# Cross-attention and table-weight FFN on one core: another source for the head norms' factor in the first batch, and the first index chunks, transfers and look-ups one place earlier

## Chip, cores and metric

The kernel runs on one core of one Trainium2 chip. The metric is device time in microseconds (us): the median over runs of the slowest core, here the only one. Lower is better.

## Reference, cut to what matters

Input x is (4, 512, 512), the context (4, 512, 256), all float32. Each batch does:

```
q  = LN_head((LN(x) @ Wq + bq) in 16 heads of 32) * w + b          # LN over the 32 values of a head
k  = LN_head(y[:496] @ Wk + bk), v = y[:496] @ Wv + bv
kd = LN_head(y[496:] @ Wkv_dca[:, :512] + b), vd = y[496:] @ Wkv_dca[:, 512:] + b   # 16 extra keys
x  = x + (softmax(q k^T / sqrt(32)) v + softmax(q kd^T / sqrt(32)) vd) @ Wo + bo
h  = silu(LN(x) @ lut[gate_idx]^T) * (LN(x) @ lut[up_idx]^T)       # lut has 16 values
x  = x + h @ lut[down_idx]^T                                        # inner size 1376
```

The FFN weights exist only as indices into a table of 16 values. The kernel looks them up once, while it works on the first batch.

## The kernel before

**Tiles and stages.** A batch has T = 4 row tiles of 128. Products use each float32 operand as a float16 high half and low half (three matmuls for one). Each engine has a program of its own, an order written out by hand; the engines meet only in counting semaphores. `core(a, ...)` is one batch of attention: projections and head norms, then stage one (scores and row maxima, slots S_ONE + 0 to 31, two slots to a *pair*), the shift (S_SUM, S_SHIFT), and stage two (transposed scores, exponentials, weighted values, slots S_TWO + 0 to 15). In later batches the FFN of the batch before fills the slots. In batch 0 there is no such FFN: `prepare(slot)` puts there what makes the FFN weights.

**Setup of batch 0.** Nine units in the order q0, q1, k1, k2, k3, d, k0, q2, q3 (`UNITS_0`; d is the extra keys of all batches in one unit of 64 rows). A unit u goes: `project(u)` on TensorE, `square(u)` on ScalarE (L865), `variance(u)` on VectorE (L1248, the sum over each head), `rstd(u)` on GpSimd (L701, the power -1/2 on 128x16 values), `normalise(u)` on VectorE (L1258), `turn_heads(u)` on TensorE (L1898, four transposes), `rescale(u)` on ScalarE (L886, L887), `low_half(u)` on VectorE (L1270). `project(u)` for u from 3 on waits for `normalise(u - 3)`, whose PSUM bank it takes. The values have `project_values(i)`. The weights are centred over each head and split on ScalarE and VectorE (L1552 makes low halves); so are the d weights, in `extra_sums`, `extra_centre`, `extra_low` (L1616, L1621, L1552) and the d context (`cd`).

**The look-ups.** The indices are 11 blocks of 3 chunks, 33 in all (`NCH`); 16 (`NQ`) is the number of stage-one pairs. A block is loaded as int32, cast to float16 on GpSimd (`convert`, L617), stored to DRAM (`store_idx`), and read back in four-fold copies (`load_rep`, L419, three buffers; `load_rep(c)` waits until `one_hot(c - 3)` is done). `one_hot(c)` is four compares on VectorE, one to a quarter (L1141), into four buffers of which each waits for the look-up before to have read it. `look_up(c)` is 32 matmuls on TensorE (L1750), eight to a quarter. `lookup_out(c)` is two copies on ScalarE (L819, L820). In stage one's pair i VectorE compares chunk i, TensorE looks up chunk i - 1 and ScalarE copies it out. In pairs 4 to 15 TensorE also makes `early` products of the next batches, which ScalarE copies out (`early_out`, L851, L854) before TensorE goes on. Chunk 15 is compared a quarter in pair 15, a quarter at S_SUM and two at S_SHIFT; TensorE looks it up in stage two's first slot, two chunks behind the compare. Chunks 31 and 32 are looked up inside the next batch's projections (`LATE`). The low half of Wo is made at S_SHIFT + 1, ahead of the compare of chunk 16 (L1552, four instructions).

**Queues.** Nearly all transfers go by SP in program order; a wait there holds back all behind it.

## Time and profile before

| | |
|---|---|
| median of 3 runs | 805.92 us (805.81 to 806.84) |
| the profiled execution | 806.87 us, its span 805.1 us |
| TensorE busy | 757.8 us of the span |
| VectorE, ScalarE, GpSimd busy | 513.0, 491.7, 264.8 us |
| mean granted TensorE clock | 0.989 |

The profile comes from one execution. Its span lies 1.8 us under that execution's own time, which lies 0.95 us over the median. Busy shares are averages over the whole span; the stages of batch 0 (roughly the first 205 us) have other limits than the rest, so they are read stage by stage.

### The profile page before, as it was taken

How to read it: one execution, taken by the hardware profiler on the slowest of the kernel's cores; microseconds unless marked ns; L12 is line 12 of the kernel's file. 1: busy time of each engine (PE TensorE's matmuls, PEld its weight loads, DVE VectorE, ACT ScalarE, POOL GpSimd, SP SyncE). 2: the span in 40 equal slices, each digit the busy share in tenths (PEclk: the TensorE clock that was granted, in tenths of full speed). 3: DMA queues.
4: the chain of work that ended last, by engine and by line, in shares of the span. 5: the costliest groups of instructions: out<-in, count | busy, mean ns of one | idle time of the engine just before them, and what ended most of it. 6: DMA issues, size and time to landing. Idle time of an engine off the chain costs nothing.

```text
span 805.1 us, 14839 instructions
## 1 busy us (share of the span) xinstructions
PE 757.8 (94%) x5833; PEld 310.6 (39%) x5833; DVE 513.0 (64%) x991; ACT 491.7 (61%) x1001; POOL 264.8 (33%) x276
## 2 busy tenths in 40 slices
PE   2888786999999999999999999999999999999998
PEld 1342232333443343324443342235433433365445
DVE  7979999898877994225769953228499800153211
ACT  3479889788646886662658866636488855511100
POOL 6883221000763321113843321035622210014320
PEclk9998999899999999999999999999999999999999
DMA  7749997586430001221500003222000000100001
GB/s 255 195 126 268 259 259 214 140 188 156 125 81 1 1 2 33 74 53 59 122 6 1 2 15 78 54 66 54 2 1 1 1 28 27 41 14 1 0 14 40
DMA packets 74389, 61.49 MB, mean 76 GB/s; under 512 B 33424, under 2 KB 60816, under 8 KB 74064
## 3 DMA queue, kind: packets, MB, share of 16 engines
q1 hardware_dynamic: 73984, 60.29, 28.2%
q8 instruction: 46, 0.75, 0.4%
q10 hardware_dynamic: 208, 0.26, 0.1%
q14 instruction: 23, 0.19, 0.1%
q0 software_dynamic: 128, 0.00, 0.0%
HBM read 43.55 MB, written 10.55 MB: 67 GB/s over the span
## 4 chain that ended last, share of the span: by engine, by line
PE 77%; DVE 13%; ACT 3%; POOL 3%; issue 3%; DVEq 0%; POOLq 0%; ACTq 0%
PE ps L1699 51%; PE ps L2050 8%; PE ps L2031 6%; PE ps L2002 5%; PE ps L1750 5%; DVE arena L1141 4%; DVE nmax L1494 3%; POOL hrstd L701 2%; PE ps L2037 2%; ACT ps L1024 2%; PE ps L1898 2%; DVE nmax L1499 1%; DVE stat L1178 1%; DVE arena L1148 1%; POOL xrstd L645 1%
## 5 line engine op out<-in xcount | busy, mean ns | idle before, releaser
L1699 PE MATMUL ps<-arena,wf_hi 128*128 128x512 f16 (+2 forms) x736 | 211.0, 371 | 0.7 <-issue 0.7
L1024 ACT ACTIVATE ps<-ps,nmax 128x496 f32<-128x496 f32 x256 | 166.1, 652 | 23.3 <-DVE nmax L1499 23.3
L1056 ACT ACTIVATE arena<-ps 128x1024 f32<-128x1024 f32 x128 | 124.3, 1026 | 72.1 <-PE ps L2037 72.1
L1699 PE MATMUL ps<-arena,wf_lo 128*128 128x512 f16 (+2 forms) x368 | 136.1, 370 | 0.0
L1699 PE MATMUL ps<-wf_hi,arena 128*128 128x512 f16 (+3 forms) x374 | 114.8, 368 | 0.5 <-DVE arena L1148 0.2
L701 POOL TENSOR_TENSOR hrstd<-hvar,mhalf 128x16 f32<-128x16 f32 (+1 forms) x33 | 100.8, 3068 | 39.5 <-DVE hvar L1248 39.4
L1699 PEld LDWEIGHTS ps<-arena,wf_hi 128*128 128x128 f16 (+1 forms) x736 | 69.5, 100 | 85.8 <-issue 21.5
L1141 DVE TENSOR_SCALAR arena<-arena,wf_lo 128x2048 f16<-128x2048 f16 (+1 forms) x132 | 89.5, 739 | 5.6 <-PE ps L1750 5.4
L1750 PE MATMUL ps<-arena,wf_lo 128*32 128x512 f16 (+1 forms) x1056 | 66.4, 396 | 13.5 <-ACT arena L851 9.5
L645 POOL TENSOR_TENSOR xrstd<-xvar,mhalf 128x1 f32<-128x1 f32 x32 | 23.8, 743 | 158.5 <-DVE xvar L1183 158.5
L1699 PE MATMUL ps<-wf_lo,arena 128*128 128x512 f16 (+3 forms) x187 | 68.5, 366 | 0.0
L2050 PE MATMUL ps<-arena 128*32 128x512 f32 x512 | 68.2, 604 | 0.0
L1699 PEld LDWEIGHTS ps<-wf_hi,arena 128*128 128x128 f16 (+1 forms) x374 | 36.4, 97 | 74.0 <-issue 39.5
L827 ACT ACTIVATE arena<-ps 128x512 f32<-128x512 f32 (+1 forms) x44 | 26.1, 594 | 62.1 <-PE ps L1699 62.1
L1499 DVE TENSOR_REDUCE nmax<-ps 128x1 f32<-128x496 f32 x96 | 63.8, 665 | 0.0
L1500 DVE TENSOR_REDUCE nmax<-ps 128x1 f32<-128x496 f32 x96 | 63.8, 665 | 0.0
L1161 DVE SCALAR_TENSOR_TENSOR arena<-ps,arena 128x512 f32<-128x512 f32 x15 | 10.4, 692 | 83.1 <-PE ps L1699 83.1
L576 POOL TENSOR_TENSOR idle<-mhalf 128x1 f32<-128x1 f32 x44 | 8.9, 202 | 151.2 <-DVE arena L1156 151.2
L2002 PE MATMUL ps<-arena 32*128 32x512 f16 x768 | 53.6, 382 | 3.6 <-ACT ps L1024 2.0
L1148 DVE SCALAR_TENSOR_TENSOR arena<-arena,ps 128x512 f32<-128x512 f32 (+1 forms) x44 | 30.0, 682 | 39.1 <-ACT arena L827 39.1
L2031 PE MATMUL ps<-arena 32*128 32x512 f16 x768 | 53.5, 381 | 0.0
L1024 ACT ACTIVATION_READ_ACCUMULATOR ps<-ps,nmax 128x1 f32 x256 | 53.3, 208 | 0.0
(154 smaller groups left out, 1049.1 us busy)
## 6 DMA issues: line engine op xcount, KB each, us to landing
arena<-idx SPq DMA_DIRECT2D x124, 128.0 KB, 3.6
arena<-in_x SPq DMA_DIRECT2D x32, 256.0 KB, 2.9
wf_lo<-in_idx SPq DMA_DIRECT2D x10, 512.0 KB, 5.3
idx<-wf_hi SPq DMA_DIRECT2D x10, 384.0 KB, 4.4
out<-arena SPq DMA_DIRECT2D x15, 256.0 KB, 2.1
wf_lo<-in_idx SPq DMA_DIRECT2D x11, 256.0 KB, 6.8
arena<-in_ctxT SPq DMA_DIRECT2D x5, 512.0 KB, 3.8
v_next<-arena SPq DMA_DIRECT2D x8, 256.0 KB, 4.5
```

The costliest lines, as they stand in the source:

```text
L701: pool.tensor_tensor(hrstd[0:n_, u % 2, :], hvar[0:n_, u % 2, :], mhalf[0:n_, :], ALU.pow).then_inc(s["hrstd_set"], 1)
L1024: last = act.activation(sc, sc, ACT.Exp, bias=nmax[:, 0, t, h:h + 1], accum_out=den[:, 0, t, h:h + 1])
L1056: act.activation(probs[n_ % 2][:, 2 * p:2 * p + 2, :], ps[:, bank:bank + 2, :], ACT.Exp).then_inc(s["probs_set"], 1)
L1141: dve.tensor_scalar(l_oh[q][:, 0:n_], l_rep[c % REPS][:, 0:n_], l_j[:, q:q + 1], None, ALU.is_equal)\
L1148: dve.scalar_tensor_tensor(out=g, in0=g, scalar=1.0, in1=ps[0:m, ffn_bank(f, it), :], op0=ALU.add, op1=ALU.mult)\
L1499: dve.tensor_reduce(nmax[:, 0, t, 2 * p:2 * p + 1], sc[:, 0:1, DCA:S], AX_X, ALU.max, negate=True).then_inc(s["max_set"], 1)
L1500: dve.tensor_reduce(nmax[:, 0, t, 2 * p + 1:2 * p + 2], sc[:, 1:2, DCA:S], AX_X, ALU.max, negate=True)\
L1699: last = pe.matmul(dst, l, r, start=(first and i == 0), stop=(stop and i == len(todo) - 1))
L1750: last = pe.matmul(ps[g * 32:(g + 1) * 32, FB + a_, 0:w], l_c[a_][:, q, :], l_oh[q][:, g * w:(g + 1) * w], start=(q == 0), stop=(q == NJ - ...
L2002: last = pe.matmul(ps[:, pair_bank(m + j // 2) + j % 2, :], qT[x_][of_head(j), g, cols], kT[y_][of_head(j), g, :], start=(k == 0), stop=(k ...
L2031: pe.matmul(ps[:, SC + j, :], kT[x_][of_head(j), g, cols], qT[y_][of_head(j), g, :], start=(k == 0), stop=False)
L2050: last = pe.matmul(ps[j * HD:(j + 1) * HD, pv_bank(g), :], v_sb[:, kt, h * HD:(h + 1) * HD], probs[n_ % 2][:, j, :], start=(kt == 0), stop ...
```

## The change

Head norms of units 0 to 6 in batch 0: VectorE takes the reciprocal of the sum (`inverse`), ScalarE the root (`root`); GpSimd keeps units 7 and 8. An `Exp` on one value stands before `rescale(7)` in ScalarE's order. The d unit is no longer split: its product is made from the float32 weights and the float32 context, and the mean over a head is taken from the product in PSUM. `one_hot(0)` moves into the setup, so every compare, look-up and copy-out of stage one handles a chunk one higher; chunk 15 is looked up at S_SHIFT, and stage two's look-ups run one chunk behind the compare. Wo is transferred once the d products are made, blocks 1 and 2 are cast and stored before the last projection, Wo's low half moves into stage two's first two slots. The written orders of the setup change on all four engines. In the diff below, calls that stand on lines of their own are joined on one line, and long arguments are cut.

```diff
-LATE = {AHEAD: NCH - 2, AHEAD + 1: NCH - 1}
+LATE = {AHEAD + 1: NCH - 1}
...
@@ SP
-            sp.wait_ge(s["wd_lo"], 1)
-            sp.dma_start(st_o..., by_chunk("Wo")).then_inc(s["wo_in"], 16)
...
             load_rep(2)
+            sp.wait_ge(s["proj_done"], UNITS_0.index(("d", 0)) + 1)
+            sp.wait_ge(s["v_done"], values_of((0, 0)).index(("d", 0)) + 1)
+            sp.dma_start(st_o..., by_chunk("Wo")).then_inc(s["wo_in"], 16)
+            store_idx(1)
+            store_idx(2)
             sp.wait_ge(s["proj_done"], nth_unit((0, 0), len(UNITS_0)))
             sp.dma_start(ctx_early...)
-            store_idx(1)
...
@@ GpSimd, setup
-                    rstd(0)
+                    norm(1, 0, (0, 0)); selectors(); norm(1, 1, (0, 0)); norm(1, 2, (0, 0))
                     convert(0)
-                    for u in range(1, len(units)):
-                        rstd(u)
+                    norm(1, 3, (0, 0))
                     convert(1)
+                    lookup_constants(); shift_patterns()
+                    convert(2)
+                    rstd(7)
+                    rstd(8)
                     low_half(a, 7, 0)
-                    convert(2, 1)
-                    context_low(2)
-                    convert(3, 3)
+                    convert(3, 2)
+                    context_low(3)
                     convert(4, 4)
                     convert(5, 5)
                     dca_shift(a, 0, 6)
                     low_half(a, 8, 6)
...
@@ ScalarE
+            def root(u):
+                n_ = MD if UNITS_0[u][0] == "d" else P
+                act.wait_ge(s["inv_set"], u + 1)
+                if u >= 2:
+                    act.wait_ge(s["qn_set"], u - 1)
+                act.activation(hrstd[0:n_, u % 2, :], hinv[0:n_, u % 2, :], ACT.Sqrt).then_inc(s["hrstd_set"], 1)
...
-                    act.activation(wd[0][:, :, :], st_d, ACT.Copy, scale=WS).then_inc(s["wd_hi"], 1)
...
+                    values(4)
+                    act.activation(warm[:, :], mhalf[:, 0:1], ACT.Exp)
                     rescale(7)
...
-                            lookup_out(c - 1)
+                            lookup_out(c)
+                if slot == S_ONE + 1:
+                    lookup_out(0)
...
                 if slot >= S_SHIFT + 1:
-                        lookup_out(c - 2)
+                        lookup_out(c - 1)
@@ VectorE
+            def inverse(u):
+                ...
+                dve.reciprocal(hinv[0:n_, u % 2, :], hvar[0:n_, u % 2, :]).then_inc(s["inv_set"], 1)
...
                     variance(a, 0)
                     context_lo(a, ctx_first, cT)
-                    value_bias(); key_low(); standardise(1, 2, ...); extra_context_low()
+                    inverse(0)
+                    moments(1, 2, a, x_first[2])
                     variance(a, 1)
                     normalise(a, 0, True)
-                    values_low(); variance(a, 2); extra_sums(); extra_centre(); parameters()
+                    inverse(1); standardise(1, 2, ...); parameters(); variance(a, 2)
                     normalise(a, 1, True)
+                    inverse(2)
                     variance(a, 3)
-                    extra_low()
                     normalise(a, 2, True)
+                    moments(1, 3, a, x_first[3]); inverse(3); variance(a, 4); inverse(4); low_half(0)
+                    normalise(a, 3, True); extra_centre(a); low_half(1); turn(1, 2, ...); standardise(1, 3, ...)
+                    low_half(2); normalise(a, 4, True); variance(a, 5); inverse(5); low_half(3)
+                    normalise(a, 5, True); turn(1, 3, ...); variance(a, 6); inverse(6); low_half(4)
+                    one_hot(0, (0,)); variance(a, 7); one_hot(0, (1,)); low_half(5); normalise(a, 6, True)
+                    one_hot(0, (2,)); (d keys into kT); variance(a, 8); value_bias(); normalise(a, 7, True)
+                    low_half(6); one_hot(0, (3,))
...
+            def extra_centre(a):
+                u = units_of(a).index(("d", 0))
+                kd_ps = heads(ps[0:MD, proj_bank(a, u), :])
+                dve.wait_ge(s["proj_done"], nth_unit(a, u + 1))
+                dve.tensor_reduce(sum_d, kd_ps, AX_X, ALU.add).then_inc(s["kd_sum"], 1)
+                dve.wait_ge(s["kd_sum"], 1)
+                dve.scalar_tensor_tensor(out=kd_ps, in0=spread(sum_d), scalar=-1.0 / HD, in1=kd_ps, ...).then_inc(s["kd_cent"], 1)
...
             def prepare(slot):
-                if slot == S_SHIFT + 1:
-                    (low half of Wo, g = 0 to 3)
                 for c in lookups_in(slot):
-                    if c < NCH - 1:
-                        one_hot(c, (0,) if c == NQ - 1 else range(NJ))
+                    if c < NQ - 2:
+                        one_hot(c + 1)
+                    elif c == NQ - 1:
+                        one_hot(c, (0,))
+                    elif NQ <= c < NCH - 1:
+                        one_hot(c)
+                if slot in (S_TWO, S_TWO + 1):
+                    (low half of Wo, two of the four g in each)
@@ TensorE
-                        keys = [(both(lambda a_: cd[a_][:, i, :]), both(lambda a_: wd[a_][:, i, 0:D])) for i in range(KC)]
+                        keys = [(ctx_dca[:, i * MD:(i + 1) * MD], st_d[:, i, 0:D]) for i in range(KC)]
...
+                    turn(1, 0, ...); turn(1, 1, ...); project(0); project(1)
+                    project_values(0)
                     project(2)
+                    project_values(1)
                     project(3)
-                    project_values(0)
                     turn(1, 2, a, LB0[2], x_first[2])
-                    project_values(1)
                     turn_heads(0)
                     project(4)
                     turn_heads(1)
-                    project_values(2)
                     project(5)
                     turn_heads(2)
+                    project_values(2); project(6); turn_heads(3)
                     project_values(3)
                     turn(1, 3, a, LB0[3], x_first[3])
-                    turn_heads(3); project(6)
                     turn_heads(4)
                     project(7)
...
                 for c in lookups_in(slot):
-                    if slot < S_SUM and c:
+                    if slot < S_SUM and c < NQ - 1:
+                        look_up(c)
+                    elif slot >= S_TWO:
                         look_up(c - 1)
-                    elif slot >= S_TWO:
-                        look_up(c - 2)
+                if slot == S_SHIFT:
+                    look_up(NQ - 1)
```

## Rows read from the trace of the kernel before

**Rows 1.** Windows of batch 0: busy time of each engine, granted clock (PEclk), DMA share, GB/s
```profile
40.00:60.00 20.00, 16.22 (x93) 8.44 (x91) 15.50 (x27) 15.25 (x28) 18.30 (x8) 0.94 0.42 123
...
100.00:120.00 20.00, 17.04 (x207) 6.26 (x206) 19.99 (x27) 17.83 (x54) 4.65 (x4) 1.00 0.97 262
...
160.00:180.00 20.00, 20.00 (x312) 7.45 (x308) 18.72 (x35) 17.49 (x26) 1.12 (x2) 1.00 0.88 184
```

**Rows 2.** Groups by line on GpSimd, 0 to 56 us
```profile
L701 POOL TENSOR_TENSOR hrstd<-hvar,mhalf 128x16 f32<-128x16 f32 (+1 forms) x9 | 29.6, 3302 | 1.4 <-DVE hvar L1248 1.3
```

**Rows 3.** Timeline of VectorE, setup and first pair: start, duration, line, idle before
```profile
24.66 1.22 DVE L1221 TENSOR_TENSOR arena<-arena 128x1024 f16<-128x1024 f32 x1
...
29.28 1.85 DVE L1552 SCALAR_TENSOR_TENSOR wv<-arena,wv 128x1024 f16<-128x1024 f32 x1
...
31.67 1.20 DVE L1616 TENSOR_REDUCE arena<-arena 128x32 f32<-128x1024 f32 x1
32.91 1.29 DVE L1621 SCALAR_TENSOR_TENSOR arena<-arena 128x512 f32<-128x512 f32 x2
...
36.20 2.28 DVE L1552 SCALAR_TENSOR_TENSOR wd<-arena,wd 128x2048 f16<-128x2048 f32 x1
...
55.67 1.19 DVE L1494 TENSOR_REDUCE nmax<-ps 128x2 f32<-128x992 f32 x1 [1.08 <-PE ps L2002]
...
61.75 2.29 DVE L1494 TENSOR_REDUCE nmax<-ps 128x2 f32<-128x992 f32 x2 [0.41 <-PE ps L2002]
```

**Rows 4.** Timeline of TensorE: products of the setup, a head turn, float32 products
```profile
27.25 1.46 PE L1699 MATMUL ps<-wk,arena 128*128 128x512 f16 x6
28.54 0.38 PE L1699 MATMUL ps<-b,sel_k 128*128 128x512 f16 x1
...
37.26 0.60 PE L1898 MATMUL ps<-ident,arena 128*128 128x128 f32 x4
...
45.65 2.75 PE L1699 MATMUL ps<-wq,arena 128*128 128x512 f16 x12
...
147.55 1.06 PE L2050 MATMUL ps<-arena 128*32 128x512 f32 x8
...
151.25 1.06 PE L2050 MATMUL ps<-arena 128*32 128x512 f32 x8
```

**Rows 5.** Timeline of ScalarE: d weights, a small copy, the table load after stage one
```profile
34.24 1.91 ACT L991 ACTIVATE wd<-arena 128x2048 f16<-128x2048 f32 x1 [0.91 <-DVE arena L1621]
...
56.90 0.20 ACT L1018 ACTIVATE arena<-ps 128x32 f32<-128x32 f32 x1 [0.64 <-DVE nmax L1494]
...
137.85 1.28 ACT L1034 ACT_TABLE_LOAD   x1
```

**Rows 6.** Timeline of TensorE, look-ups of stage one
```profile
61.57 3.25 PE L1750 MATMUL ps<-arena,wf_lo 128*32 128x512 f16 x32
...
88.98 1.91 PE L1750 MATMUL ps<-arena,wf_lo 128*32 128x512 f16 x32 [2.23 <-ACT arena L851]
...
129.80 1.91 PE L1750 MATMUL ps<-arena,wf_lo 128*32 128x512 f16 x32 [0.90 <-ACT arena L851]
...
134.78 1.91 PE L1750 MATMUL ps<-arena,wf_lo 128*32 128x512 f16 x32 [0.90 <-ACT arena L851]
```

**Rows 7.** Timeline of ScalarE, the copy-out of the third early product
```profile
88.33 0.60 ACT L851 ACTIVATE arena<-ps 128x512 f32<-128x512 f32 x1 [1.22 <-POOL arena L666]
```

**Rows 8.** Timeline of VectorE: a chunk's compare, a standardise, the next batch's first residual
```profile
130.65 2.73 DVE L1141 TENSOR_SCALAR arena<-arena,wf_lo 128x2048 f16<-128x2048 f16 x4
...
175.77 0.55 DVE L1188 TENSOR_SCALAR arena<-arena,mv,xrstd 128x512 f32<-128x512 f32 x1 [0.67 <-POOL xrstd L645]
...
210.43 0.69 DVE L1215 SCALAR_TENSOR_TENSOR arena<-ps,arena 128x512 f32<-128x512 f32 x1 [0.54 <-PE ps L1699]
```

**Rows 9.** Timeline of TensorE, the first FFN product of the next batch
```profile
232.06 0.59 PE L1699 MATMUL ps<-arena,wf_hi 128*128 128x512 f16 x2 [0.74 <-issue]
```

**Rows 10.** Windows of TensorE around the shift: busy time, granted clock, DMA share, GB/s
```profile
139.00:146.00 7.00, 5.03 (x48) 0.53 0.41 116
```

204 lines of the change are left out of this document (106 added, 98 removed).

## Prediction

> **What bounds the kernel now.** I read the busy times of windows first, because every edit lies in batch 0 and the page's shares are means over all batches. Three limits follow each other. In the setup (to 55.67 us, the first row maximum [rows 3]) no engine is full but GpSimd: 18.3 of 20 us between 40 and 60, against 15.5 on VectorE, 15.25 on ScalarE, 16.2 on TensorE [rows 1]. The groups by line say with what: nine powers for the head norms, 3.3 us each, 29.6 us together [rows 2]. In stage one VectorE is full (19.99 of 20), with ScalarE at 17.8 and TensorE at 17.0 close behind [rows 1]. From stage two on TensorE is full (20.00 of 20), VectorE at 18.7 [rows 1]. What ends the setup or stage one sooner therefore moves all that comes later; what takes work from VectorE in stage two is worth nothing; what takes TensorE work out of stage two or the next batch is worth its length, unless something else is late there.
>
> **Setup: the powers.** Seven of nine go from GpSimd to a reciprocal and a root. No row shows either. For the reciprocal the rows bound it between 0.1 us (next to nothing on 16 values) and 0.6 (half the reduce over 1024 values, 1.20 [rows 3]); I take 0.15, seven make 1.0. The root works on 16 values and stands between nothing and the 0.20 of the copy of 32 [rows 5]; I take 0.15. The GpSimd queue (7 x 3.3 = 23 us in a row) is then gone, and the question is what is late next. Two lists compete, TensorE's and VectorE's, both from the moment the context's low half is made: 24.66 + 1.22 = 25.9 now [rows 3]. In the new order nearly the same instructions stand ahead of it (two moments fewer, about 1.0 each; the low halves of values and keys more, 1.1 each), so I keep 25.9 to 26.3.
>
> TensorE, from there: a product of six float16 matmuls takes 28.54 - 27.25 = 1.3, with the bias 1.5; one of twelve 2.75, with bias 2.8 less overlap; four head transposes 0.60, of which 0.44 count when others follow [rows 4]. The d product becomes float32. Float32 matmuls of 512 columns show only four side by side, a quarter of the array each: 1.06, less the 0.17 of tail that 1.46 has over 1.29, 0.89 [rows 4]. One that fills the array takes 0.22 if those four run one after another and 0.89 if they run at once; I take 0.88, so two are 1.76 in place of 1.3, for keys and values each. The other bound makes the d unit 2.6 us cheaper than that. The list: four value products 5.2, four key products 6.0, two queries 5.6, d 1.97 + 1.76, two turns 0.9, eight head turns 3.5: 24.9 us. It ends at 26.1 + 24.9 = 51.0, and with the scores (0.8) the first maximum is at 51.8 at the soonest.
>
> VectorE, from there: eight variances and eight normalises at 0.6 (9.7), seven reciprocals 1.0, two moments 2.0, two standardises 0.9, parameters 0.9, seven low halves 3.9, the d mean in PSUM 1.25, two turns 1.2, the four compares of chunk 0 at 2.73 / 4 = 0.68 less overlap [rows 8] 2.65, copies 0.3: 23.9 us, so 49.8 without a wait. What left it: 1.20 + 1.29 + 2.28 for the d weights [rows 3] and 0.3 for the d context. ScalarE loses 1.91 [rows 5] and gains seven roots and two table loads. Walking the three orders together, VectorE waits 1.1 for the square of unit 3 (TensorE has that product at 26.1 + 1.3 + 1.5 + 1.3 + 1.5 = 31.7) and about 1.5 for units 7 and 8, and TensorE never waits longer than 0.5: both lists meet at 52.5. Blocks 1 and 2 are now cast on GpSimd inside the setup, beside VectorE: the one cast there now made the values' low half 1.85 where an instruction of the same size took 1.22 [rows 3]. Two more casts and the pattern copies cost 0 to 2.5 by this; some fall beside PSUM reads, I take 0.5. The first maximum: 53.0 in place of 55.67, **-2.7 us**. Bounds: 51.8 (-3.9) and, if VectorE's waits and collisions add instead of hiding each other, 55.0 (-0.7).
>
> The Trainium skill (ScalarE: Activation LUTs, "What ACT_TABLE_LOAD costs") puts a switch of table set at 2.66 us with its drain. The trace has 1.28 for the load [rows 5]. The first switch falls in a gap of ScalarE of 2.6 us either way; the second, ahead of `rescale(7)`, would by the page cost the first pair 1.4 us more and make the sum 1.4 smaller.
>
> **First pair.** `look_up(0)` now stands between the last head turn and the second scores. Maximum to next maximum is 61.75 - 55.67 = 6.1 us with a wait of 0.41 for the scores, which themselves waited for `rescale(8)` [rows 3]. If the look-up takes 1.91 it hides there (-0.4); at the clock that the first look-up has now, 3.25 [rows 6], compares and scores come 1.5 later. I take 0.
>
> **Stage one, a chunk higher.** The compare, the look-up and the copy-out keep their distances, so a pair is what it was. VectorE loses a whole chunk (2.73) in the fifteenth pair. That is not 2.7 us: look-ups start 134.78 - 129.80 = 4.98 us apart, TensorE waiting 0.90 for ScalarE's early copy each time [rows 6], and this loop (look-up, copy-out, exponentials, early copy, next look-up) is as long as VectorE's own pair. At the end ScalarE's last exponentials and the table load at 137.85 [rows 5] gate the shift as now. Value of the missing compare: **0**, at most -0.5.
>
> One stall goes. The third early copy waits 1.22 us on ScalarE for GpSimd's low half of unit 8 [rows 7], which stands behind `dca_shift(a, 0, 6)`: six chunks compared. TensorE therefore waits 2.23 instead of 0.90 before the look-up at 88.98 [rows 6]. Six chunks are now compared one pair (about 4.9 us) sooner, which covers the 1.22 fully: **-1.35 us**. The waits at later chunks keep their slots.
>
> **The sixteenth chunk and stage two.** `look_up(15)` goes from stage two into the shift, where TensorE is idle anyway. In stage two 16 look-ups stay, one of them of 384 columns instead of 512 (-0.4), and in the next batch's projections the look-up of chunk 31 (1.4 us) goes. There the gain is not whole: before the first FFN product TensorE already waits 0.74 [rows 9] for the transposed rows, at the end of a VectorE list without a gap but one, 0.54 before its first residual [rows 8]. TensorE can only win what that list wins: -0.55.
>
> Against it: with one chunk of lead instead of two, VectorE must finish the compare for slot n + 1 while it has its other work of slot n. A slot is 151.25 - 147.55 = 3.70 us [rows 4]; a chunk 2.65; a standardise comes 0.67 late after GpSimd [rows 8]. Counting slot by slot (a compare may start 2.4 us into the slot and must start by 4.3), slots 1, 4 and 10, where a standardise stands ahead of the compare, and the two with Wo's low halves (1.25 each) miss it, by 0.4 + 0.15 + 0.6 + 0.5 = 1.7. Stage two's present waits (0.5, from the same standardises) go: +1.2. Bounds 0 and, if each slot missed by 0.3, +4.8. Stage two: -0.4 + 1.2 = **+0.8**, the next batch **-0.55**.
>
> **The clock.** From 139 to 146 the granted clock is 0.53 [rows 10], nearly 1.2 GHz, after TensorE had stood idle for the shift; slot 0's products pay 2.4 us for it (a look-up 3.25 against 1.91 [rows 6] is 1.35 of that). The new order puts 1.8 us of look-up, in four pieces, into that idle time. I do not count on it: 0, bound -2.4.
>
> **Transfers.** Wo (1 MB), blocks 1 to 4 and a context now queue on SP between 42 and 50 us; ScalarE wants the context in the first pair. The present queue at 40 to 60 is at 0.42 of the engines [rows 1]; cover is the rest. 0, and 1 us if the context lands late.
>
> **Sum.** -2.7 + 0 - 1.35 + 0.8 - 0.55 = -3.8. The profiled execution took 806.87 us (span 805.1); it should take 803.1. The median, 0.95 below it, goes from 805.92 to **802.1**.
>
> **Rivals.**
> A, the clock holds: `look_up(15)` keeps TensorE at 2.4 GHz through the shift. -3.8 - 2.4: 799.7. For it: its four pieces leave no gap over 1.5 us. Against: 1.8 us of look-up in about 7 from the last early product to the shift's transposes. 0.13.
> B, the setup is not GpSimd's: VectorE's list with casts and waits ends at 55, the lead lost in stage two costs 2 to 3. -0.7 - 1.35 + 2 - 0.55 = -0.6: 805.3. For it: three engines at 15 to 16 of 20 [rows 1], and the 0.6 us that one cast cost VectorE [rows 3]. 0.15. The Trainium skill (SBUF — State Buffer, "SBUF: two separate sides") says that of a VectorE instruction with two SBUF inputs and a GpSimd instruction the later one is locked out until the other is done; the trace agrees (1.85 against 1.22). By that rule casts placed beside VectorE's list are dear, and it is what B would come from.
> C, slower: the table thrashes. If square, copy or identity is not in the root's table set, each of roots 0 to 6 brings a load before and after. The point from which it decides is the first square after a root. Twelve loads of 1.28 [rows 5] in place of two are 12.8 us more on an engine with about 10 idle between 23 and 54, and each root stands in the chain to a normalise: +8 on the setup. -3.8 + 8: 810.1. Against: squares and copies now run beside exponentials with no load between. 0.07. The Trainium skill (ScalarE: Activation LUTs, "Table sets: the hidden batching unit") puts exponential and root in different sets and asks to batch calls by set; it also has the cheap functions in every set, which speaks against C.
> That the change does not do what it says (the powers stay in the chain): units 7 and 8 are still powers; if `normalise(8)` became the end it would cost under 1 us, inside the forecast.
>
> **Chances and range.** Forecast 0.65, A 0.13, B 0.15, C 0.07. The range reaches past A to 799.2 (0.5 of the 1.2 that the setup's best bound has over its value), and to 806.2 past B (0.9 more of stage two's bound); outside are C and the tails. The forecast's own range is 800.5 to 804.5. A change of 0.2% (1.6 us) is about what a measurement tells. Faster by more (below 804.3): the forecast but for its upper tail 0.60, A 0.13, B 0.05: 0.78. Within: 0.12. Slower (C and a bad stage two): 0.10.
>
> **What would show it.** First row maximum at 52 to 54 (right), 55 or later (B). No GpSimd power before unit 7. One table load before the first root and one before `rescale(7)`, not more (else C). The third early copy without a wait for GpSimd. Look-ups 4.98 apart in pairs 5 to 15. Short waits of TensorE for compares in slots 1, 4 and 10, each under 1 us; if every slot has one, the stage two term is wrong. The wait before the first FFN product grows from 0.74 to about 1.6. The granted clock at the shift near 0.5 (else A). The forecast fails if the setup's float32 products take over 1.76 a pair, or if the reciprocal is over 0.3.

## The result, and the profile after

The changed kernel takes 808.3 us (median of 18 runs, 806.32 to 809.16); the kernel before, run beside it on the same chip, 806.52 us (18 runs, 805.30 to 807.96). The ratio is 1.0018, interval [1.0012, 1.0024]. Forecast were 802.1 us and a range up to 806.2: the time moved the other way and lies outside the range. The profiled execution took 809.01 us, with a span of 807.2 us and a mean granted clock of 0.992.

The points below are starts of the same instruction in both traces; they add up to the two spans (us).

| stretch | before | after | difference | forecast |
|---|---|---|---|---|
| start to first row maximum | 55.67 | 56.89 | +1.22 | -2.7 |
| first to second row maximum | 6.08 | 8.00 | +1.92 | 0 |
| second maximum to the shift's transposes | 79.22 | 77.91 | -1.31 | -1.35 |
| transposes to the scores of stage two's second slot | 5.61 | 4.37 | -1.24 | 0 |
| second slot to the next batch's first query product | 56.42 | 58.86 | +2.44 | +0.8 |
| that product to the first FFN product | 29.06 | 28.31 | -0.75 | -0.55 |
| first FFN product to the end | 573.04 | 572.86 | -0.18 | 0 |
| sum | 805.1 | 807.2 | +2.1 | -3.8 |

The windows of the changed kernel that answer to [rows 1] and [rows 10] (busy time of TensorE, its weight loads, VectorE, ScalarE, GpSimd, then granted clock, DMA share, GB/s):

```profile
40.00:60.00 20.00, 17.25 (x97) 8.42 (x99) 18.87 (x33) 16.30 (x32) 13.78 (x12) 0.95 0.84 235
...
160.00:180.00 20.00, 19.90 (x300) 6.89 (x296) 18.35 (x34) 17.23 (x26) 1.12 (x2) 1.00 1.06 185
...
139.00:146.00 7.00, 5.69 (x64) 1.59 (x68) 6.06 (x14) 5.54 (x10) 0.00 (x0) 0.76 0.41 112
```

In the setup GpSimd went from 18.3 to 13.8 of 20 us and VectorE from 15.5 to 18.9: the fullest engine is another one now. In stage two TensorE is at 19.90 instead of 20.00.

TensorE's timeline says more (start, duration, line; in brackets the idle time before and who ended it):

```profile
27.66 2.72 PE L1725 MATMUL ps<-wv,arena 128*128 128x512 f16 x6 [3.33 <-DVE arena L1241]
30.17 1.68 PE L1725 MATMUL ps<-wk,arena 128*128 128x512 f16 x6
...
37.62 1.93 PE L1725 MATMUL ps<-arena 128*64 128x512 f32 x4
...
58.74 1.12 PE L1924 MATMUL ps<-ident,arena 128*128 128x128 f32 x4 [1.95 <-DVE arena L1285]
59.78 3.60 PE L1776 MATMUL ps<-arena,wf_lo 128*32 128x512 f16 x32
```

and its windows in the same columns as above:

```profile
26.00:28.00 2.00, 0.34 (x1) 0.14 (x2) 2.00 (x4) 0.59 (x3) 0.00 (x0) 0.80 0.00 0
28.00:30.00 2.00, 2.00 (x6) 0.73 (x5) 1.92 (x8) 0.41 (x1) 1.29 (x2) 0.50 0.01 4
...
58.00:60.00 2.00, 1.26 (x8) 0.86 (x12) 1.78 (x3) 1.73 (x7) 1.16 (x1) 0.50 1.10 290
```

Twice TensorE stands idle, 3.33 and 1.95 us, and twice the granted clock is then 0.50, that is 1.2 GHz. The first value product takes 2.72 us where its like in [rows 4] took 1.46, the key product behind it 1.68, and the look-up that was moved between turn and scores takes 3.60.

The same places in the trace of before:

```profile
24.19 2.76 PE L1699 MATMUL ps<-wq,arena 128*128 128x512 f16 x12 [0.90 <-DVE arena L1206]
...
57.52 1.12 PE L1898 MATMUL ps<-ident,arena 128*128 128x128 f32 x4 [1.95 <-DVE arena L1258]
60.17 1.47 PE L2002 MATMUL ps<-arena 32*128 32x512 f16 x12 [1.54 <-ACT arena L887]
...
143.31 3.33 PE L1750 MATMUL ps<-arena,wf_lo 128*32 128x512 f16 x32
```

There the second query product filled the time up to the first key product at 27.25; in the first pair TensorE idled just as long, but the second scores (60.17) stood ahead of the look-up; and the look-up of stage two's slot 0 took 3.33.

VectorE in the same stretch, beside GpSimd's casts:

```profile
27.43 0.25 DVE L1275 RECIPROCAL hinv<-hvar 128x16 f32<-128x16 f32 x1
...
35.54 0.70 DVE L1268 TENSOR_REDUCE hvar<-arena 128x16 f32<-128x528 f32 x1 [1.35 <-ACT arena L870]
...
38.83 1.61 DVE L1297 TENSOR_TENSOR arena<-arena 128x512 f16<-128x512 f32 x1
...
46.02 1.14 DVE L1297 TENSOR_TENSOR arena<-arena 128x512 f16<-128x512 f32 x1
...
56.89 1.19 DVE L1529 TENSOR_REDUCE nmax<-ps 128x2 f32<-128x992 f32 x1 [0.42 <-PE ps L2032]
...
64.89 2.29 DVE L1529 TENSOR_REDUCE nmax<-ps 128x2 f32<-128x992 f32 x2 [0.69 <-PE ps L2032]
```

```profile
38.43 1.46 POOL L620 CAST wf_hi<-wf_lo 128x1536 f16<-128x1536 int32 x1
...
45.16 1.46 POOL L620 CAST wf_hi<-wf_lo 128x1536 f16<-128x1536 int32 x1
```

The low half of a unit is one instruction (L1297), mostly of 0.68 us; it takes 1.61 and 1.14 where a cast of GpSimd lies beside it. From 36 to 56 us VectorE waits only once, for 0.39 us.

ScalarE's tables, and the third early copy (before: [rows 7]):

```profile
25.01 1.28 ACT L878 ACT_TABLE_LOAD   x1
27.71 0.22 ACT L878 ACTIVATE hrstd<-hinv 128x16 f32<-128x16 f32 x1 [1.41 <-DVE hinv L1275]
...
55.34 1.28 ACT L1028 ACT_TABLE_LOAD   x1
56.64 0.20 ACT L1028 ACTIVATE warm<-mhalf 128x1 f32<-128x1 f32 x1
...
90.10 0.65 ACT L854 ACTIVATE arena<-ps 128x512 f32<-128x512 f32 x1
```

Besides a load at 3.67 us that both kernels have, the setup has these two loads, none between roots and squares. The third early copy no longer waits. TensorE's look-ups then show the stall leave, stage two pay, and the next batch's wait grow (before: [rows 6, 9]):

```profile
90.80 1.91 PE L1776 MATMUL ps<-arena,wf_lo 128*32 128x512 f16 x32 [0.90 <-ACT arena L854]
...
144.65 2.51 PE L1776 MATMUL ps<-arena,wf_lo 128*32 128x512 f16 x32 [0.30 <-DVE arena L1161]
...
153.38 2.51 PE L1776 MATMUL ps<-arena,wf_lo 128*32 128x512 f16 x32 [0.48 <-DVE arena L1161]
...
234.34 0.59 PE L1725 MATMUL ps<-arena,wf_hi 128*128 128x512 f16 x2 [1.52 <-issue]
```

At a granted clock of 1.00 a look-up of 32 products takes 1.91; 2.51 is one that waits inside for the quarters of a compare (in slot 2 the compare ends at 155.23, the look-up at 155.89). Slots 0, 2, 5 and 11 have 2.51, slots 3, 9 and 13 have 2.06 to 2.16. VectorE shows what stands ahead of such a compare:

```profile
152.03 0.55 DVE L1208 TENSOR_SCALAR arena<-arena,mv,xrstd 128x512 f32<-128x512 f32 x1 [0.67 <-POOL xrstd L648]
152.49 2.74 DVE L1161 TENSOR_SCALAR arena<-arena,wf_lo 128x2048 f16<-128x2048 f16 x4
```

### The profile page after: what moved, and what is told of

Read it like the earlier page. It is cut to its first block, busy times and chain, and to the rows that moved or that the text cites. A ratio compares the mean times of both kernels' runs of the same rounds, so it can differ in the third digit from the quotient of the medians.

```text
span 807.2 us, 14844 instructions
## 1 busy us (share of the span) xinstructions
PE 759.8 (94%) x5829; PEld 308.6 (38%) x5829; DVE 512.3 (63%) x995; ACT 494.1 (61%) x1010; POOL 238.7 (30%) x269
## 4 chain that ended last, share of the span: by engine, by line
PE 71%; DVE 17%; ACT 5%; issue 3%; DMA 2%; POOL 1%; SPq 1%; DVEq 0%
PE ps L1725 50%; PE ps L2080 7%; DVE arena L1161 6%; PE ps L2061 5%; PE ps L2032 5%; ACT ps L1042 2%; DVE nmax L1529 2%; PE ps L1776 2%; PE ps L2067 1%; PE ps L1924 1%; DMA arena<-in_x 1%; DVE stat L1198 1%; DMA v_next<-arena 1%; DVE nmax L1534 1%; DVE hvar L1268 1%
## 5 line engine op out<-in xcount | busy, mean ns | idle before, releaser
L706 POOL TENSOR_TENSOR hrstd<-hvar,mhalf 128x16 f32<-128x16 f32 x26 | 76.7, 2964 | 45.9 <-DVE hvar L1268 45.6
L648 POOL TENSOR_TENSOR xrstd<-xvar,mhalf 128x1 f32<-128x1 f32 x32 | 20.1, 629 | 179.8 <-DVE xvar L1203 179.8
L830 ACT ACTIVATE arena<-ps 128x512 f32<-128x512 f32 (+1 forms) x44 | 26.1, 594 | 63.0 <-PE ps L1725 63.0
```

The lines of the kernel that those rows point to most:

```text
L706: pool.tensor_tensor(hrstd[0:n_, u % 2, :], hvar[0:n_, u % 2, :], mhalf[0:n_, :], ALU.pow).then_inc(s["hrstd_set"], 1)
```

## The experiments

Ratios are to the kernel before in the same session. "Filler" is a product of float16 weights into a bank that nobody reads then; it adds work and no result. Runs of one kernel spread over 2 to 3 us, so a difference of one trace is set against the medians.

| run | median us | ratio to before, interval |
|---|---|---|
| changed kernel | 808.30 | 1.0018 [1.0012, 1.0024] |
| e1 filler in the first pair | 806.53 | 0.9994 [0.9985, 1.0004] |
| e4 filler in the setup | 805.79 | 0.9986 [0.9977, 0.9995] |
| e6 both | 804.70 | 0.9978 [0.9969, 0.9987] |
| e3 stage two in the old order | 807.38 | 1.0003 [0.9993, 1.0013] |
| e2 powers in the new order | 820.44 | 1.0167 [1.0152, 1.0182] |
| b2 roots in the old order | 813.26 | 1.0089 [1.0074, 1.0104] |
| e5 constants early | 807.33 | 1.0012 [1.0002, 1.0021] |
| b1 five chunks, before | 806.15 | 0.9992 [0.9984, 1.0001] |
| b3 fillers before, misplaced | 812.50 | 1.0077 [1.0063, 1.0091] |
| b4 fillers before | 804.69 | 0.9980 [0.9971, 0.9989] |
| b5 b4 and five chunks | 804.37 | 0.9975 [0.9965, 0.9985] |
| c1 first combination | 803.51 | 0.9969 [0.9956, 0.9981] |
| c2 second combination | 801.95 | 0.9947 [0.9934, 0.9959] |
| c3 c2 and constants early | 802.46 | 0.9951 [0.9937, 0.9965] |

### The clock in the first pair (e1), in the setup (e4), both (e6)

```diff
                     project(1)
+                    for k_ in range(14):        # e4 and e6
+                        pe.matmul(ps[:, FB, :], wq[0][:, k_ % KQ, 0:P], wq[0][:, k_ % KQ, :], start=True, stop=True)
                     project_values(0)
...
                     if prev is None and m == 0:
+                        for k_ in range(9):     # e1 and e6
+                            pe.matmul(ps[:, FB + 1, :], wq[0][:, k_ % KQ, 0:P], wq[0][:, k_ % KQ, :], start=True, stop=True)
                         turn_heads(8)
```

> The changed kernel with nine float16 matmuls of no use put on TensorE between the first scores and the head turn of unit 8, into bank 7, where it stood idle for 1.95 us. Theory (clock): the second row maximum comes 8.0 us after the first because the look-up of chunk 0, now on the path, runs at 1.2 GHz (3.60 us) after that idle time; kept busy, the look-up takes 1.91 and the distance falls to 6.1 to 6.5, the time by 1.5 to 1.9 us. Rival (order): the look-up ahead of the second scores costs the same wherever the clock stands, distance 7.5 or more, time changed by less than 0.5 us.

> The changed kernel with fourteen float16 matmuls of no use on TensorE (bank 6) in its idle 3.3 us before the first value product. Theory (clock): that product takes 1.46 instead of 2.72 us, squares 2 and 3 come 1.4 us sooner, VectorE's waits of 0.91 and 1.35 us for them shrink, and the first row maximum comes at 55.5 instead of 56.89. Rival (VectorE's list): its list is full from 36 us on and takes the waits back, so that the maximum stays at 56.5 to 56.9 and the time as it is.

> The changed kernel with both fillers at once: 14 products without a use while TensorE waits ahead of the first value product, and 9 between the first scores and the turn of unit 8. Theory (TensorE's clock, which falls after each of the two waits, carries 1.4 us of the setup and 1.9 us of the first pair, and the two are independent): the gains add. First value product to first row maximum 27.8 us, first to second maximum 5.9, later stages as in the changed kernel; against the changed kernel -3.2, so 804.6 to 805.2 where the kernel before has 806.9: ratio 0.9975. Rival (a filler only moves a wait: VectorE's list ends the setup, and what TensorE wins in one place it waits in the next): first maximum not before 55.5, ratio 0.999 to 1.000.

TensorE's timeline in e1, then in e4:

```profile
55.75 2.12 PE L2043 MATMUL ps<-wq 128*128 128x512 f16 x9
57.77 0.66 PE L1924 MATMUL ps<-ident,arena 128*128 128x128 f32 x4
58.35 1.91 PE L1776 MATMUL ps<-arena,wf_lo 128*32 128x512 f16 x32
```

```profile
23.36 3.19 PE L1961 MATMUL ps<-wq 128*128 128x512 f16 x14
26.86 1.45 PE L1725 MATMUL ps<-wv,arena 128*128 128x512 f16 x6 [0.31 <-DVE arena L1241]
```

In e1 the turn takes 0.66 instead of 1.12, the look-up 1.91 instead of 3.60, and first to second maximum is 5.83 instead of 8.00 us (6.08 before): the first pair's loss is the clock. In e4 the first value product takes 1.45, and from it to the first maximum it is 27.78 us instead of 29.23. With both (e6) it is 27.78 and 5.83 again. So in the traces the two add, and the rival (won in one place, waited out in the next) falls. The medians lie 1.8, 2.5 and, with both, 3.6 us under the changed kernel's, which agrees within their spread. Extra work made the kernel faster.

What the clock leaves of the setup shows in e6, from the end of the context's low half to the end of VectorE's last compare of the setup (columns as in the windows above):

```profile
26.62:54.22 27.60, 26.58 (x139) 13.01 (x139) 25.93 (x55) 19.33 (x37) 15.56 (x15) 1.00 0.79 213
```

Of 27.60 us TensorE is busy 26.58 and VectorE 25.93. Both lists are full, and both are longer than the 24.9 and 23.9 us that the prediction gave them: VectorE's takes 26.3, and TensorE, from the first value product (26.85) to the first scores (53.70), is busy 26.06.

### Stage two in the old order (e3)

```diff
-LATE = {AHEAD + 1: NCH - 1}
+LATE = {AHEAD: NCH - 2, AHEAD + 1: NCH - 1}
...
                     elif slot >= S_TWO:
-                        look_up(c - 1)
+                        look_up(c - 2)
-                if slot == S_SHIFT:
-                    look_up(NQ - 1)
```

with the copy-outs one chunk later too, and Wo's low half back at S_SHIFT + 1.

> The changed kernel with stage two as before: chunk 15 looked up in its first slot, two chunks behind the compare, chunk 31 in the next batch, Wo's low half before the compare of chunk 16. Theory: the waits for late compares (2.4 us over the slots) go, the clock falls at the shift again (+1.2 us), and the next batch gets its 0.75 back: 0.5 us less in all. Rival (the lost lead costs nothing, the waits are there anyway): 1 to 2 us more.

```profile
141.96 0.58 PE L2049 MATMUL ps<-ident_h,caug 128*128 128x128 f16 x4 [7.10 <-DVE caug L1557]
...
144.30 2.59 PE L1776 MATMUL ps<-arena,wf_lo 128*32 128x512 f16 x32
...
148.68 1.91 PE L1776 MATMUL ps<-arena,wf_lo 128*32 128x512 f16 x32
```

Transposes to the next batch's first query product take 61.30 us here, 63.23 in the changed kernel and 62.03 before; from there to the first FFN product it is 0.77 us longer than in the changed kernel. The slots behind slot 0 have no late compare. The part moved in stage two costs about 1 us net, more than the +0.25 forecast for stage two and next batch together (+0.8 - 0.55) and more than the 0.5 expected of this run; its rival (1 to 2 us slower) falls. Slot 0 has to be read with care: its look-up took 3.33 in the trace of before, 2.59 here, and 2.60 in b1, which does the same as before there. The whole stretch is 5.61 in before and 4.71 in b1, so 0.7 to 0.9 us of its -1.24 is the spread from one execution to another.

### The norms alone: powers in the new order (e2), roots in the old one (b2)

```diff
# e2: in the changed kernel
-                    inverse(0) ... inverse(6)          (VectorE)
-                    root(0) ... root(6)                (ScalarE)
+                    rstd(0) ... rstd(6)                (GpSimd, among its norms and casts)
# b2: in the kernel before
                     variance(a, u)
+                    inverse(u)                         (VectorE, u = 0 to 6)
...
                     square(a, 3, True)
+                    root(2)                            (ScalarE, likewise the others)
-                    rstd(0); for u in range(1, len(units)): rstd(u)     (GpSimd)
+                    rstd(7); rstd(8)
```

> The changed kernel with the head norms of units 0 to 6 back as powers on GpSimd, without reciprocals, roots and the second table load; everything else, the order of VectorE's list too, as changed. Theory: the powers, seven of 3.3 us with casts and constants among them, are a queue of about 28 us from 27 us on, the first row maximum comes at 59 to 61, the time is 2 to 4 us more. Rival (the setup is bound by the other engines in the new order): it stays within 1 us of 56.9.

> The kernel before with one part of the change alone: the factor of units 0 to 6 by VectorE's reciprocal and ScalarE's root, in the old orders of the engines (units 7 and 8 stay powers; an Exp on one value stands ahead of the rescale of unit 7). The d unit, the compare of chunk 0, the transfers, the shift and stage two are as before. Theory (the nine powers were what ended the setup, 3.3 us apart; in the changed kernel it was the clock's fall after TensorE's idle 3.3 us and a full VectorE list of 26.3 us that took the gain): here VectorE has no compare of chunk 0 and TensorE no gap ahead of its key products, so the first row maximum comes at 53.5 to 54.5 where the kernel before has 55.7, the rest as before: ratio 0.998. Rival (the powers bound nothing, they were hidden behind the two other lists): first maximum 55.5 to 57, as VectorE has 1.8 us more in its list; ratio 1.000 to 1.002.

Both were misses: e2 lies 12 us over the changed kernel and b2 7 us over the kernel before, where +2 to +4 and -1.6 were expected. The waits of VectorE in the setup, of e2 and then of b2 (who waited for whom: total, times, longest):

```profile
DVE arena L1284 <- POOL hrstd L706: 11.0, 6, 2.8
DVE arena L1284 <- issue: 2.2, 1, 2.2
```

```profile
DVE arena L1294 <- ACT arena L896: 3.8, 3, 1.6
DVE hvar L1265 <- ACT arena L867: 3.5, 1, 3.5
```

In e2 VectorE waits for a power ahead of a normalise six times. GpSimd's list is why: from its first head-norm power to its last it is busy 37.91 of 42.73 us (25.67 to 68.40), where before it was busy 30.95 of 31.45 (24.82 to 56.27). The nine powers are the same, but the changed order puts three casts, two norms of x and the look-up constants among them; the old order had one cast there. The first seven with what stands among them were expected to take 28 us and took 33.7 (25.67 to 59.35), and the last two came behind one more cast. In b2 a root puts ScalarE itself into the chain: ScalarE waits for a reciprocal (1.82, 2.22 and 1.18 us), and the rescales queued behind the root are what VectorE then waits for. Where I put the roots among ScalarE's work was my choice, and a better place may exist; it was not tried. What is shown: the root is no gain in the old order as I placed it, the new order is none without the root, and only the two together come near the time of before.

### GpSimd beside VectorE (e5)

```diff
                     norm(1, 1, (0, 0))
+                    lookup_constants()
+                    shift_patterns()
                     norm(1, 2, (0, 0))
                     convert(0)
                     norm(1, 3, (0, 0))
                     convert(1)
-                    lookup_constants()
-                    shift_patterns()
```

> The changed kernel with one step moved on GpSimd: its look-up constants and shift patterns come ahead of the norms of tiles 2 and 3 and of the first two casts, so that from 36 to 50 us GpSimd has less beside VectorE. Theory (collisions of VectorE's copies with GpSimd's cost the setup about 1 us: 1.61 and 1.14 us where such instructions take 0.68): the pattern copies run beside VectorE's earlier, looser stretch, first maximum 0.5 to 1.0 earlier than in the changed kernel, ratio to it 0.999. Rival (the casts, not the patterns, collide, and they only come later now; the norm of tile 2 comes 3 us later and holds the query products back): first maximum the same or up to 1.5 us later, first value product later than 27.7, the time 0 to +1.5.

VectorE's low halves in e5:

```profile
38.88 1.61 DVE L1297 TENSOR_TENSOR arena<-arena 128x512 f16<-128x512 f32 x1
...
46.06 0.62 DVE L1297 TENSOR_TENSOR arena<-arena 128x512 f16<-128x512 f32 x1
```

The one at 46 us lost its 0.5 us of collision, the one at 38.9 (beside a cast) kept its 0.9. First value product to first maximum went from 29.23 to 28.99 (e1 and e3, without this edit, have 29.07 and 29.17). In the median e5 cannot be told from the changed kernel (the intervals overlap). The combination c1 shows where the rest goes: against e6 this stretch is 27.39 instead of 27.78, but the first value product starts at 27.25 instead of 26.85, because the standardise at 12.14, now beside GpSimd's constants and pattern copies, takes 0.94 instead of 0.54. The first maximum is at 54.64 in c1 and 54.63 in e6. The collision was moved, not removed, and the rival is nearer to what happened.

### The sixth chunk alone (b1)

```diff
-                    dca_shift(a, 0, 6)
-                    low_half(a, 8, 6)
+                    dca_shift(a, 0, 5)
+                    low_half(a, 8, 5)
```

> The kernel before with one step alone: GpSimd shifts and splits five chunks of unit 7 and 8 ahead of the early copy instead of six. Theory (ScalarE's third early copy waits 1.22 us for that step, and TensorE then 2.23 instead of 0.90): that wait is gone, second maximum to shift 1.3 us shorter (77.9 where the kernel before has 79.2), all else as before: ratio 0.9984. Rival (the sixth chunk comes late elsewhere, or the gain belongs to the chunks that moved up): 0 to +1, ratio 1.000 or above.

```profile
87.27 1.91 PE L1750 MATMUL ps<-arena,wf_lo 128*32 128x512 f16 x32 [0.90 <-ACT arena L851]
...
93.76 1.91 PE L1750 MATMUL ps<-arena,wf_lo 128*32 128x512 f16 x32 [1.84 <-ACT arena L851]
```

The stall at the third early copy is gone (0.90 instead of 2.23), but the next look-up comes 6.49 us later where it came 5.93 later before. Second maximum to transposes is 78.47 instead of 79.22: 0.75 of the 1.3 us that the whole change has there. The median moved by 0.4 us, which the interval does not separate from nothing; 1.3 us had been expected.

### Fillers in the kernel before (b3, b4, b5)

```diff
                 between(S_SHIFT)
+                pe.wait_ge(s["l_out"], NQ - 1)          # b3, 28 fillers in bank FB
+                pe.wait_ge(s["S_exp"], NS - 2)          # b4 and b5 instead, 18 fillers in bank TB
+                for k_ in range(28): ...
                 pe.wait_ge(s["S_exp"], nth(a, NS, NS))
```

and the 9 fillers of e1. b5 has the five chunks of b1 as well.

> The kernel before with fillers alone: 9 products without a use between the first scores and the turn of unit 8, and 28 ahead of the shift's transposes. It asks what the clock is worth without the change. Theory (before, the first pair hid the low clock behind VectorE's compare of chunk 0, so nothing is to be had there; only the shift pays, slot 0 at 5.1 us with a look-up of 3.3): first maximum 55.7, first to second maximum 5.8 to 6.1, transposes to second slot 3.8 to 4.1 instead of 5.6; 804.3 to 805.0, ratio 0.998. So the change with its clock held (the second combination, 801.95) keeps 2.5 to 3 us over this. Rival (the change brings nothing once the clock is taken out of both): 802 to 802.8, ratio 0.9955.

> The kernel before with fillers alone, in another place than the run before: 9 products without a use between the first scores and the turn of unit 8, and 18 right behind the sixteenth pair's look-up, in a bank that the exponentials have left, where TensorE idles 4.3 us ahead of the shift's transposes. Theory (the clock costs the old order about 2.2 us at the shift: from the transposes to the second slot 5.6 us, and 3.4 in the run before; and about 0.4 in the first pair, where VectorE's compare covers it): transposes at 140.4 to 140.7, second slot 3.4 to 3.8 later, 804.0 to 804.8, ratio 0.9975 to 0.998; the changed kernel with its clock held (801.95) then keeps 2 to 3 us from its own parts. Rival (the clock is all there is): 802.0 to 802.8, ratio 0.995 to 0.996.

> The kernel before with the fillers of b4 and GpSimd's early step on five chunks instead of six. Theory (the step alone took 0.75 us off stage one in its own run): 0.7 to 1.3 below b4, 803.0 to 804.0, ratio 0.9965; what is then left to the changed kernel with its clock held is 1 to 2 us, of setup and index order. Rival (the gain was the chance of that one run's profile): as b4, ratio 0.998.

TensorE in b3, then in b4:

```profile
140.38 7.90 PE L2021 MATMUL ps<-wq 128*128 128x512 f16 x28 [3.88 <-ACT wf_hi L820]
148.12 0.39 PE L2025 MATMUL ps<-ident_h,caug 128*128 128x128 f16 x4
```

```profile
137.73 4.06 PE L2021 MATMUL ps<-wq 128*128 128x512 f16 x18
142.08 0.38 PE L2025 MATMUL ps<-ident_h,caug 128*128 128x128 f16 x4 [0.29 <-DVE caug L1522]
...
143.36 1.91 PE L1750 MATMUL ps<-arena,wf_lo 128*32 128x512 f16 x32
```

b3 is my mistake: in the old order the copy that its fillers wait for comes only behind the shift, so they started when TensorE should have been done, and held the transposes back by some 7 us. It says nothing on its question. b4 puts them into the idle time: transposes to second slot 3.4 us instead of 5.6, first to second maximum 5.60 instead of 6.08, and 1.65 us off the median. That is what the clock costs in these two places of the kernel before. In b4's own trace the transposes come at 142.08, not at 140.4 to 140.7 as expected, because the look-up behind the third early copy, at 88.47, took 3.52 us. b5 takes the wait ahead of that look-up away (second maximum to transposes 78.85 instead of 80.82 in the two traces), but its median is only 0.3 us under b4's: short of the 0.7 expected, and with overlapping intervals, so nearer to its rival.

### The combinations (c1, c2, c3)

c1 is e6 with e5's edit and e3's; c2 is e6 with e3's edit and, as in b3, 28 fillers ahead of the shift's transposes (here the copy-out comes early enough); c3 is c2 with e5's edit.

> The changed kernel with four edits: both fillers of the clock, GpSimd's constants early, and stage two with the last index chunks in the old order (look-ups two chunks behind the compare, Wo's low half ahead of stage two). Theory: the fillers give 3.2 us, stage two in the old order 1.2, the constants 0 to 0.8, and they add, as they lie in different stages: 808.3 - 4.4 to 5.2 = 803.1 to 803.9, below the kernel before by 0.4% (ratio 0.996). Rival (the clock falls at the shift in any case once stage two is in the old order, and the gain of 1.2 is not on top of the fillers'): 804.5 to 805.3, ratio 0.9975, as with the two fillers alone.

> The changed kernel with both fillers of the setup and first pair, stage two and the last index chunks in the old order (GpSimd's constants where the changed kernel has them), and a third filler: 28 products without a use ahead of the shift's transposes, where TensorE idles 7.1 us in the combination before. Theory (slot 0 of stage two pays for the clock at 1.2 GHz after that idle time): granted clock near 1.0 at the shift, look-up of slot 0 at 1.9 instead of 2.57 us, transposes to second slot 3.8 instead of 4.85 us, so 1.0 to 1.5 us below the combination: 802.0 to 802.8, ratio to the kernel before 0.995. Rival (the fillers end before the transposes and TensorE waits for the shift's copies again, or they end late and hold the transposes back): slot 0 as in the combination or the transposes later, 803.5 to 804.5, ratio 0.997.

> The second combination (three fillers, stage two and the last index chunks in the old order) with GpSimd's constants early as well. Theory: the value from first value product to first maximum is 27.4 instead of 27.7, all else as in the second combination: 801.5 to 801.9, ratio 0.9943. Rival: the first value product starts 0.4 later with the constants early, as in the first combination, and the gain is gone: 801.9 to 802.4, ratio 0.9947.

TensorE in c2, and its window around the shift:

```profile
132.17 6.22 PE L2053 MATMUL ps<-wq 128*128 128x512 f16 x28 [0.90 <-ACT arena L854]
138.35 0.38 PE L2057 MATMUL ps<-ident_h,caug 128*128 128x128 f16 x4
...
139.64 1.91 PE L1776 MATMUL ps<-arena,wf_lo 128*32 128x512 f16 x32
```

```profile
139.00:146.00 7.00, 6.81 (x116) 2.60 (x108) 6.93 (x12) 5.34 (x7) 0.00 (x0) 1.00 0.40 106
```

c1 came as expected. c2 came just below its range: 801.95, 4.2 us under the kernel before and 6.4 under the changed one, the fastest version here. With the clock held in both orders, 801.95 stands against 804.69 (b4), or 0.9947 against 0.9980: the change's own parts, without its stage two, are worth 2 to 3 us. Against b5 (0.9975), which has the sixth chunk's part of them, 2.3 us are left. c2 has one filler more than b4, in the setup, where the trace of before has no gap ahead of its key product [rows 4]. c3 went as its rival said: 802.46, the first value product at 27.75 instead of 26.85 (0.41 of it a wait for x) and nothing gained over c2.

## Why the prediction was wrong

**"I keep 25.9 to 26.3" and the lists behind it: the step that failed first.** The new order makes the queries ready sooner, so the second query product ended at 24.33 us instead of 27.17; with both done, TensorE had nothing left and idled 3.33 us for VectorE's low half of the context. I counted its list from the end of that wait and never asked what it had done before. The two products behind that ran at 1.2 GHz, the second in part: 1.4 us (e4). The clock had a paragraph of its own, but only for the shift. The start itself was 0.7 us late too: the first value product comes at 26.85 in e4 and e6, for 26.1. The new order has VectorE wait 0.68 us for GpSimd ahead of the first standardise (at 7.09), where the old one had other work.

**VectorE's list.** Given 23.9 us, it took 26.3 in e6 (26.62 to 54.22, less waits of 0.91 and 0.39). Three terms carry it, read from start to start. Seven low halves took 5.3 us instead of 3.9, two of them beside casts. Seven reciprocals took 1.1 for 1.0 (0.16 apart), but a variance with a reciprocal behind it takes 0.72 instead of 0.61. Two standardises took 1.4 instead of 0.9. The collisions were costed at 0.5 us and came to about 2: 0.9 and 0.5 on two low halves, 0.5 on a standardise. Against that, VectorE's waits were 1.3 us where 2.6 were forecast. First value product to first maximum is then 27.8 us in e6, where the forecast had 26.9 (53.0 - 26.1): 0.9 more. The Trainium skill (SBUF — State Buffer, "SBUF: two separate sides") has the lock-out that the prediction weighed; the 1.61 us beside the cast at 38.43 agrees with it. It was rival B's mechanism, and it acted, together with a clock that B did not have.

**Float32 products.** Costed at 1.76 a pair; the keys' pair (four records) takes 1.77 from its start to the next product (37.62 to 39.39), the values' pair 1.86 (43.53 to 45.39): as forecast within 0.1. The 1.93 of the row includes the tail of the last product.

**The trace itself.** The changed kernel's profiled execution started its list 0.8 us late: VectorE waited 0.71 us for a tile of x at 8.94, which e3 did not (its first value product starts at 26.86, its first maximum at 56.03). Of the nine other traces with the changed order, seven have no such wait and two have 0.19 and 0.41. So the setup is +0.4 rather than +1.2 in most of the traces.

**First pair, forecast 0.** The bound of +1.5 for a look-up at 1.2 GHz stood in the text, and I took the other end. The rows held the answer: the old look-up of 3.25 in [rows 6] was slow after the same wait of 1.95 us (and one of 1.54). Before, the second scores (60.17) stood ahead of the look-up and came while VectorE compared chunk 0 (58.48 to 61.34), and the look-up ran beside the second maxima. So the low clock cost at most 0.5 us (6.08, with fillers 5.60 in b4). The change moved that compare away and put the look-up ahead of the second scores, which VectorE waits for: it took the cover off. With fillers (e1) the distance is 2.2 us shorter; 1.9 of that lay over the forecast.

**Stage one.** The stall (-1.31 for -1.35), the fifteenth pair's missing compare (worth 0), the distance of 4.98 us: right. The cause was only half right: b1 has 0.75 of it by the sixth chunk alone; the rest came with the other moves of index blocks, and which of them was not separated.

**Stage two, forecast +0.8.** The mechanism was right, the size not: seven slots were late, not five; six of them lie in this stretch and lose 0.15 to 1.26 us each, together 3.4 instead of 1.7; less the 0.5 of before and 0.4 of shorter look-up, +2.44. The slots behind a standardise, which I had named, lose most: 1.26, 0.75 and 0.72 us (look-ups of slots 2, 5 and 11). I let a compare start as late as 4.3 us into its slot because the look-up takes it in quarters. That was about 0.25 too generous: the compare at 179.52 starts 4.30 us behind the scores of its slot, and the look-up it feeds takes 2.16 for 1.91. And I did not count that VectorE makes a low half of the weighted values ahead of some compares, where it waits for ScalarE's high half (0.83 us ahead of slot 9's compare, 0.99 ahead of slot 13's).

**Clock at the shift, forecast 0 with -2.4 as rival A.** The window from 139 to 146 went from 0.53 to 0.76, part of A. Against b1's execution of the old order the stretch won 0.3 us, against before's 1.24; b4 and c2 show what all of it is worth, 2.2 us in that stretch.

**Next batch.** -0.75 for -0.55, and the wait ahead of the first FFN product grew to 1.52 as forecast.

**Rival C.** Only the two loads forecast appeared. The Trainium skill (ScalarE: Activation LUTs, "What ACT_TABLE_LOAD costs") adds a drain to the load; here the copy before the load ends at 55.33, the load starts at 55.34 and the Exp at 56.64, so no drain shows on either side of it, and the extra 1.4 us that the page would have put on the first pair is not there.

In all, the missing 5.9 us (from -3.8 to +2.1) are the clock in setup and first pair, 1.4 and 1.9; in the setup also the late tile of x, 0.8, the late start, 0.7, and VectorE's longer list, 0.9; and stage two's compares, 1.6; less 1.24 at the shift and 0.3 in the other stretches. The clock's two terms and stage two's are shown by undoing them (e1, e4, e3); the list and the late start are read from the traces.

## What to carry to other kernels

A product list is not done when it is summed: look for the idle time that a new order opens ahead of it, and price what follows at the clock that the trace shows after a gap of that length, as a range where the traces differ. A slow instruction that costs nothing may be slow under cover; before moving the cover away, find its duration in the trace and put it into the sum. A factor that takes a detour over another engine belongs to the order around it, so neither is to be costed alone.

## What the hardware showed beside that

- Work without a use in TensorE's gaps made this kernel faster: 14 and 9 products took 3.6 us off the changed kernel's median, and 28 more, with stage two reordered, another 2.8.
- After TensorE's idle 1.95 us in the first pair (in before and b1 with a second wait of 1.54 and 1.63) the first look-up took 3.25 us before, 3.60 in the changed kernel, 2.94 in e5 and 3.61 in b1 instead of 1.91: the clock fell each time, not for equally long. After the 2.23 us ahead of the third early copy it held in the trace of before (a look-up of 1.91, [rows 6]) and had fallen in b4's (3.52 for the same look-up). A gap of some 2 us is so a risk rather than a price. And a fall can be free: a look-up at about 70 us, behind a wait of 0.66, took 3.38 before, 3.37 in e1, 3.43 in e6 and 1.91 in the changed kernel (at 74.01), and second maximum to transposes is 78.00 in e1 and 77.91 in e6 as in the changed kernel.
- VectorE's reciprocal of 128x16 values takes 0.25 us alone and 0.16 from start to start; ScalarE's root of the same 0.21. GpSimd's power on them takes 2.9 to 3.9.
- The same code at the shift showed a look-up of 3.33 us in one execution (before) and 2.60 in another (b1): 0.7 us of a trace's difference there is chance.
